# Second softmax pass of an audio tower: bias written into PSUM ahead of the score matmuls, exponential read from PSUM

## The chip, the cores and the metric
One core of one Trainium2 chip runs the whole kernel. The metric is device time in microseconds. Engine names are those of the profile: PE is TensorE's matmul, PEld its weight load, DVE is VectorE, ACT is ScalarE, POOL is GpSimd, SP is the engine that issues most DMAs.

## The reference, cut to what matters
The input x has shape (16, 256, 128): 16 batches. A convolution over 5 time steps gives 252 rows of 256 features per batch; then comes an attention layer with 16 heads of width 16, a learned bias by relative position and a causal mask; then a quantised feed-forward layer. The change touches the attention alone:

```
sim = einsum('bhid,bhjd->bhij', q, k) * scale
sim = sim + bias                  # rel_emb[bucket(j - i)], one 252 x 252 table per head
sim = where(causal_mask, mask_value, sim)
attn = softmax(sim, axis=-1)
out = einsum('bhij,bhjd->bhid', attn, v)
```

The same bias table serves all 16 batches.

## The kernel before
The kernel has three stages in time: a preparation of weights and bias tables (to about 60 us), the convolution and attention of all batches (about 60 to 535 us), and the feed-forward layer (the rest). The first and last are the same in both kernels.

The attention stage is a software pipeline with one **body** per batch, numbered b = -3 to 16. Every engine runs its own list of steps per body, in order: `PE_ORDER` (L439), `DVE_ORDER` (L446), `ACT_ORDER` (L450). A step is a name, an offset and a part; the offset says which batch it works on: `("k", 1, 0)` in body b computes the first half of the k projection of batch b + 1, `("conv", 2, ...)` the convolution of batch b + 2. A step whose batch does not exist is left out, so the bodies at both ends are thinner: body 15 has no P1, q, k, v or conv.

The scores are computed twice. The **first pass** (P1, 12 pieces of 504 columns, for batch b + 1) has queries on partitions. PE puts the bias in with a matmul against an identity and adds q times k (L616, L619), and DVE takes row maxima out of PSUM (`mx`, L758). The maxima are transposed (step mT, L627), negated on ACT (step mneg, L866), and sent by a DMA into row 65 of the stacked q (L961). The **second pass** (P2, 12 pieces, for batch b) has keys on partitions, and that row makes each score come out less its maximum. For each piece PE computes the scores (L637), DVE adds the bias table `biasT` and writes the sum to the SBUF buffer `sbr`, which has four slots (L749), and ACT takes the exponential of `sbr` into `pt` (L834). The step PV (L650, L654) multiplies three pieces of `pt` by v. P2[0] to P2[5] stand at the start of a body, P2[6] to P2[11] at its end.

P1 and P2 pieces share four PSUM banks in turn, in PE's order. Before PE writes a piece, `score_free` (L510) waits until the engine that read the bank four pieces earlier is done: the maximum for a P1 piece, the addition for a P2 piece. Other steps share one more ring of single banks; among them x2T (L690) uses the bank of mT and so waits for mneg.

From the maxima runs this loop round to the next body: P1[11], mT, mneg, DMA, P2[0] on PE, the k projection behind it on PE (L596), its high and low parts kh on ACT (L876) and kl on DVE (L789), three DMAs into the stacked k (L946), and P1[0] of the next batch, which waits for all six DMAs of q and k. On ACT, kh stands behind P2[0], which stands behind everything from the end of the body before: `xh`, `xnh`, `osb`, `xn2`, P2[6], mneg, P2[7], P2[8], `x2`, P2[9], qh, P2[10], `osb`, P2[11].

Step `ax` (L815) takes the largest magnitude of a batch of finished features. In the kernel before no ordinary body has it: one stands behind each of the 12 P2 additions of body 15, and four stand in body 16.

Of the kernel before, what the change touches and what calls it, by code (L numbers as in the profile page):

```python
# [25 lines left out]
ALU = mybir.AluOpType  # L26
# [38 lines left out]
def audio_tower(nc, x, cw, cb, gamma, beta, rmean, rvar, wq, wk, wv, wo, bo, rel, wg, wu, wd, hot, out):  # L65
    with ExitStack() as ctx:
# [3 lines left out]
        def sem(name):  # L70
# [22 lines left out]
            lines_dram bias_in anti_r antib_r flipT_ps flipN_ps biasT_r biasN_r vec_ready cbx_r vec_in ident pool_init dve_init act_init  # L93
            x_in xT_ps xh_r xl_r conv_ps relu_r v1_r h_r hb_r bns_r mv_r ve_r rstd_r nb_r xn_r
            xnT_ps xnh_r xnl_r q_ps k_ps v_ps qh_r ql_r kh_r kl_r va_r stack_in
            p1_ps mx_r mT_ps mneg_r mneg_in p2_ps sb_r exp_r pv_ps osb_r oT_ps rc_r on_r onT_ps onh_r onl_r
            wo_ps h2_r spilled bns2_r mv2_r ve2_r rstd2_r nb2_r nm2_r nm_r xn2_r x2T_ps x2_r ax_r
            xi_r xqh_r xq_r ag_r ared par sc_r ap_r ao_r oq_r oh_r ol_r""".split()
        names += [n + str(i) for n in "g_ps g_r u_ps raw_r raw_out raw_in gq_r sig_r sq_r p_r au_r uq_r g2_r o_r".split()
# [28 lines left out]
        def sba(name, shape, dt=F32):  # L128
            return sb(name, shape, dt, pa)
# [291 lines left out]
        xn, xn2 = sba("xn", [128, 2, C]), sba("xn2", [128, 2, C])  # L421
        xnh, xnl = sba("xnh", [128, KT, N], F16), sba("xnl", [128, KT, N], F16)
        mx = sba("mx", [128, 2, H])
        sbr = sba("sbr", [128, 4, 2 * N])
        pt = sba("pt", [128, 2, 3, 2 * N])
        osb = sba("osb", [128, G, N])
        rc = sba("rc", [128, 2, H])
# [7 lines left out]
        def pieces(kind, off, first, end):  # L435
            return [(kind, off, n) for n in range(first, end)]
# [6 lines left out]
                    ("wo", -1, 1), P1[8], ("v", 1, 1), P1[9], P1[10], ("xT", 3, 0), P1[11], ("PV", 0, 1), ("xnT", 2, 0),  # L443
                    P2[6], P2[7], P2[8], ("mT", 1, 0), ("q", 2, 0), P2[9], ("x2T", -1, 0), P2[10], ("q", 2, 1),
                    P2[11], ("PV", 0, 2)]
        DVE_ORDER = [P2[0], P2[1], ("kl", 1), P2[2], P2[3], P2[4], P2[5], ("on", -1, 0), P1[0], ("on", -1, 1),  # L446
                     P1[1], P1[2], P1[3], P1[4], ("onl", -1), P1[5], P1[6],
                     ("stats", 2), P1[7], ("h2", -1), P1[8], P1[9], ("stats2", -1), P1[10], ("xl", 3), P1[11],
                     ("xnl", 2), P2[6], P2[7], P2[8], P2[9], P2[10], ("ql", 2), P2[11]]
        ACT_ORDER = [P2[0], ("kh", 1), P2[1], ("osb", -1, 3), P2[2], P2[3], P2[4], P2[5], ("osb", 0, 0),  # L450
                     ("relu", 2), ("onh", -1), ("xn", 2), ("va", 1), ("xh", 3), ("xnh", 2), ("osb", 0, 1), ("xn2", -1),
                     P2[6], ("mneg", 1), P2[7], P2[8], ("x2", -1), P2[9], ("qh", 2), P2[10], ("osb", 0, 2), P2[11]]


# [3 lines left out]
        FF_ACT = {(-1, ("relu", 2)): [("ffhi", 0, j) for j in range(6)],  # L458
                  (-1, ("xn", 2)): [("ffhi", 0, j) for j in range(6, FF_BANKS - 1)],
                  (-1, ("va", 1)): [("ffhi", 0, FF_BANKS - 1)]}  # L460
        for c in range(12):
            FF_DVE[B - 1, P2[c]] = [("ax", c - B + 1)]
        for c, at in zip(range(12, B), (("on", -1, 1), ("onl", -1), ("h2", -1), ("stats2", -1))):
            FF_DVE[B, at] = [("ax", c - B)]
        FF_PE = {(-1, P1[2]): [("ffT", 0, 0), ("ffT", 0, 1)]}
        for j in range(FF_BANKS):
            FF_DVE[-1, P1[j + 2]] = [("fflo", 0, j)]
# [42 lines left out]
        def score_free(pe, st, b):  # L510

            i = PIECES.index(st) - 4
            for back in range(5):
                while i >= 0:
                    kind, off, n = PIECES[i]
                    if runs(b - back if isinstance(b, int) else b, off):
                        return wait(pe, "sb_r" if kind == "P2" else "mx_r", 12 * (b - back + off) + n + 1)
                    i -= 4
                i += len(PIECES)

        def piece_heads(n):

# [16 lines left out]
        def pe_step(pe, b, par):  # L539
            odd = 1 - par  # L540
            for st in step_order(PE_ORDER, FF_PE, b):
# [88 lines left out]
                elif name == "P2":  # L630
                    if part == 0:
                        wait(pe, "mneg_in", 16 * (c + 1))
                    score_free(pe, st, b)
                    heads, w = piece_heads(part)
                    kt = slice(TT, N) if w == TT else slice(0, TT)
                    for n, hd in enumerate(heads):
                        last = nc.tensor.matmul(ps[0:TT, score_bank[name, part], n * w:(n + 1) * w],  # L637
                                                kS[par][0:P2_ROWS, hd, kt], qS[par][0:P2_ROWS, hd, N - w:N],
                                                start=True, stop=True)
                    last.then_inc(S["p2_ps"], 1)  # L640
                elif name == "PV":
                    g, vc = part, va[odd if off else par]
                    if isinstance(c, int) and c == 0:
                        wait(pe, "ff_lo", FF_BANKS)
                    wait(pe, "exp_r", 12 * c + 3 * (g + 1))
                    wait(pe, "va_r", c + 1)
                    wait(pe, "osb_r", 4 * c + g - 1)
                    p = pt[0:TT, g % 2]
                    for i in range(4):
                        nc.tensor.matmul(ps[32 * i:32 * i + 32, OB + g % 2, 0:N], vc[0:TT, 0, 4 * g + i, :],  # L650
                                         p[:, i // 2, (i % 2) * N:(i % 2) * N + N], start=True, stop=True,
                                         skip_group_check=True)
                    for i in range(4):
                        last = nc.tensor.matmul(ps[32 * i:32 * i + 32, OB + g % 2, TT:N],  # L654
                                                vc[0:TT, 1, 4 * g + i, :], p[:, 2, i * TT:(i + 1) * TT],
                                                start=False, stop=True, skip_group_check=True)
                    last.then_inc(S["pv_ps"], 1)
                elif name in ("OT0", "OT1"):
                    t = int(name[2])
                    wait(pe, "osb_r", 4 * (c + 1))  # L660
                    misc_free(pe, name, b)
                    for g in range(G):
                        last = nc.tensor.transpose(bank[0:TT, g * 128:(g + 1) * 128],  # L663
                                                   osb[:, g, t * TT:(t + 1) * TT], identf[:])
                    last.then_inc(S["oT_ps"], 1)
                elif name == "onT":
                    wait(pe, "on_r", 2 * (c + 1))
                    misc_free(pe, name, b)
                    for k in range(KT):
                        for t in range(2):  # L670
                            last = nc.tensor.transpose(bank[:, k * N + t * TT:k * N + (t + 1) * TT],
                                                       on[0:TT, t, k * 128:(k + 1) * 128], identf[0:TT, 0:TT])
                    last.then_inc(S["onT_ps"], 1)
                elif name == "wo":
                    if part == 0:
                        wait(pe, "onh_r", c + 1)
                        wait(pe, "onl_r", c + 1)
                        misc_free(pe, name, b)
                    rows = slice(part * TT, (part + 1) * TT)
                    last = three(bank[0:TT, part * C:(part + 1) * C],  # L680
                                 [((onh[:, k, rows], onl[:, k, rows]), (woT[:, 0, k], woT[:, 1, k]))
                                  for k in range(KT)])
                    if part == 1:
                        last.then_inc(S["wo_ps"], 1)
                elif name == "x2T":
                    wait(pe, "xn2_r", 2 * (c + 1))
                    misc_free(pe, name, b)
                    for k in range(KT):
                        for t in range(2):
                            last = nc.tensor.transpose(bank[:, k * N + t * TT:k * N + (t + 1) * TT],  # L690
                                                       xn2[0:TT, t, k * 128:(k + 1) * 128], identf[0:TT, 0:TT])
                    last.then_inc(S["x2T_ps"], 1)
# [15 lines left out]
        def dve_step(dve, b, par):  # L708
            for st in step_order(DVE_ORDER, FF_DVE, b):
# [28 lines left out]
                elif name == "fflo":  # L738
# [2 lines left out]
                    nc.vector.scalar_tensor_tensor(bank_dst(group, 1)[0], ps[:, OB + st[2] % 2, :],  # L741
                                                   winv[:, group[0][4]:group[0][4] + 1], bank_dst(group, 0)[0],
                                                   ALU.mult, ALU.subtract).then_inc(S["ff_lo"], 1)
                elif name == "P2":
                    n = st[2]
                    heads, w = piece_heads(n)
                    wait(dve, "p2_ps", 12 * c + n + 1)
                    wait(dve, "exp_r", 12 * c + n - 3)
                    nc.vector.tensor_tensor(sbr[0:TT, n % 4].rearrange("p (h w) -> p h w", w=w),  # L749
                                            ps[0:TT, score_bank[name, n], 0:2 * N].rearrange("p (h w) -> p h w", w=w),  # L750
                                            biasT[0:TT, heads[0]:heads[-1] + 1, 0:w], ALU.add).then_inc(S["sb_r"], 1)
                elif name == "P1":
                    n = st[2]
                    heads, w = piece_heads(n)
# [64 lines left out]
        def act_step(act, b, par):  # L819
            odd = 1 - par  # L820
            for st in step_order(ACT_ORDER, FF_ACT, b):
# [7 lines left out]
                                         scale=winv[:, group[0][4]:group[0][4] + 1]).then_inc(S["ff_hi"], 1)  # L829
                elif name == "P2":  # L830
                    n = st[2]
                    wait(act, "sb_r", 12 * c + n + 1)
                    wait(act, "pv_ps", 4 * c + n // 3 - 1)
                    nc.scalar.activation(pt[0:TT, n // 3 % 2, n % 3], sbr[0:TT, n % 4], ACT.Exp  # L834
                                         ).then_inc(S["exp_r"], 1)
                elif name == "osb":
                    g = st[2]
                    wait(act, "pv_ps", 4 * c + g + 1)
# [619 lines left out]
```

## Time and profile before

| | us |
|---|---|
| median of 3 runs | 842.63 |
| range of the runs | 839.97 to 850.68 |
| profiled execution | 847.05 |
| its span, first to last instruction | 845.2 |

Over the span PE is busy 73%, DVE 72%, ACT 51%, POOL 22%. These shares are means over stages with different limits: between 100 and 480 us PE is busy 9 tenths or more of nearly every slice, while between 490 and 535 us no engine is.

### The profile page before, as it was taken

What the parts mean: (1) busy time and instruction counts of PE and PEld (TensorE: products, weight loads), DVE (VectorE), ACT (ScalarE), POOL (GpSimd) and SP (SyncE); (2) the same over time, 40 slices, a digit from 0 to 9 for tenths busy, and PEclk for the clock granted to TensorE, in tenths of its full rate; (3) what the DMA queues carried; (4) which work ended last, traced back from release to release, by engine and by line L of the source; (5) the groups of instructions that cost most, each with busy time, mean ns of one, the idle gap of its engine ahead of it and who ended that gap; (6) DMA issues with size and microseconds to landing.
All of it is one profiled execution on the core that took longest, in us unless ns stands there. A gap on an engine that the chain in (4) does not pass through costs nothing. (4 is left out here: it accounts for less than half of the span.)

```text
span 845.2 us, 15311 instructions
## 1 busy us (share of the span) xinstructions
PE 617.8 (73%) x5162; PEld 463.7 (55%) x5162; DVE 610.1 (72%) x949; ACT 432.7 (51%) x622; POOL 187.6 (22%) x239
## 2 busy tenths in 40 slices
PE   2535699899999999999999865399997720002998
PEld 1224577778777777787777643144443300002998
DVE  5736777778887788887788756256679995995442
ACT  0510444666545665545665343144498862444772
POOL 1320222112221122221122000000035552650000
PEclk9976999999999999999999865599999975555999
DMA  6333023232133331233321200000043302661343
GB/s 169 100 124 44 15 32 58 45 58 42 29 56 44 56 56 31 38 56 44 56 48 27 41 1 12 13 0 0 0 170 158 149 37 73 219 220 49 115 131 98
DMA packets 40063, 57.37 MB, mean 68 GB/s; under 512 B 5820, under 2 KB 31868, under 8 KB 40028
## 3 DMA queue, kind: packets, MB, share of 16 engines
q1 hardware_dynamic: 38876, 56.13, 26.7%
q10 hardware_dynamic: 1152, 0.79, 0.5%
q8 instruction: 20, 0.33, 0.2%
q14 instruction: 15, 0.12, 0.1%
HBM read 25.06 MB, written 19.13 MB: 52 GB/s over the span
## 5 line engine op out<-in xcount | busy, mean ns | idle before, releaser
L758 DVE TENSOR_REDUCE mx<-ps 126x2 f32<-126x504 f32 (+1 forms) x192 | 125.1, 675 | 45.0 <-PE ps L619 44.5
L1406 PE MATMUL ps<-wdT,oh 128*126 128x256 f16 x384 | 65.7, 279 | 93.6 <-DVE ol L1366 93.6
L834 ACT ACTIVATE pt<-sbr 126x504 f32<-126x504 f32 x192 | 115.1, 617 | 30.5 <-DVE sbr L749 29.3
L749 DVE TENSOR_TENSOR sbr<-ps,biasT 126x504 f32<-126x504 f32 x192 | 120.6, 674 | 9.9 <-PE ps L637 9.3
L1406 PEld LDWEIGHTS ps<-wdT,oh 128*126 128x126 f16 x384 | 48.6, 140 | 94.5 <-DVE ol L1366 94.5
L616 PE MATMUL ps<-biasN,identb 126*126 126x504 bf16 x192 | 75.2, 392 | 21.1 <-DMA k_st<-kl 21.1
L910 POOL TENSOR_TENSOR h<-h,bc 126x512 f32<-126x512 f32 x16 | 20.3, 1268 | 273.5 <-ACT h L850 273.5
L619 PE MATMUL ps<-k_st,q_st 65*126 65x252 f16 (+1 forms) x512 | 75.3, 249 | 0.0
L1077 PE MATMUL ps<-x2t,wgT 128*128 (+1 forms) x288 | 63.9, 387 | 11.0 <-DVE x2t L1120 11.0
L1077 PE MATMUL ps<-x2t,wuT 128*128 (+1 forms) x288 | 63.4, 376 | 11.2 <-ACT raw L1246 11.1
L637 PE MATMUL ps<-q_st,k_st 66*126 66x252 f16 (+1 forms) x512 | 67.5, 252 | 3.3 <-DMA q_st<-mneg 3.3
L619 PEld LDWEIGHTS ps<-k_st,q_st 65*126 65x126 f16 x512 | 60.9, 140 | 16.0 <-issue 1.5
L573 PE MATMUL ps<-wcT,xh 128*126 128x256 f16 x320 | 62.2, 279 | 0.0
L637 PEld LDWEIGHTS ps<-q_st,k_st 66*126 66x126 f16 x512 | 50.6, 139 | 11.2 <-issue 6.2
L861 ACT ACTIVATE xn<-h,nb,rstd 126x256 f32<-126x256 f32 x32 | 17.5, 593 | 72.7 <-POOL nb L904 72.7
L1077 PEld LDWEIGHTS ps<-x2t,wgT 128*128 128x128 f16 x288 | 28.7, 100 | 46.0 <-DVE x2t L1120 11.4
L1406 PE MATMUL ps<-wdT,ol 128*126 128x256 f16 x192 | 53.5, 279 | 0.0
L1077 PEld LDWEIGHTS ps<-x2t,wuT 128*128 128x128 f16 x288 | 27.6, 98 | 46.8 <-issue 9.0
L1284 POOL TENSOR_SCALAR sq<-sig 128x1512 int32<-128x1512 f32 x16 | 44.1, 2759 | 39.2 <-ACT sig L1255 32.2
L841 ACT ACTIVATE osb<-ps 128x252 f32<-128x252 f32 x64 | 23.7, 370 | 52.7 <-PE ps L663 43.2
L1266 ACT ACTIVATE g<-gat,sc 128x1512 int16 (+1 forms) x16 | 24.8, 1554 | 44.5 <-DVE gat L1183 33.0
L573 PE MATMUL ps<-wcT,xl 128*126 128x256 f16 x160 | 44.9, 281 | 0.0
(181 smaller groups left out, 1430.5 us busy)
## 6 DMA issues: line engine op xcount, KB each, us to landing
up_raw<-raw SPq DMA_DIRECT2D x14, 756.0 KB, 3.2
raw<-up_raw SPq DMA_DIRECT2D x14, 756.0 KB, 4.3
q_st<-qh SPq DMA_DIRECT2D x32, 128.0 KB, 3.9
k_st<-kh SPq DMA_DIRECT2D x32, 128.0 KB, 4.0
res<-hall SPq DMA_DIRECT2D x16, 252.0 KB
hin<-res SPq DMA_DIRECT2D x16, 252.0 KB
out<-y SPq DMA_DIRECT2D x16, 252.0 KB
xin<-in_x SPq DMA_DIRECT2D x16, 128.0 KB, 3.7
```

Of the source, the lines that this page charges most:

```text
L573: last = nc.tensor.matmul(bank[0:TT, t * C:(t + 1) * C], *products[i], start=False, stop=(i == 14))
L616: nc.tensor.matmul(dst, identb[0:TT, 0:TT], biasN[0:TT, heads[0]:heads[-1] + 1, N - w:N], start=True, stop=True)
L619: last = nc.tensor.matmul(dst[:, n * w:(n + 1) * w], qS[odd][0:P1_ROWS, hd, qt], kS[odd][0:P1_ROWS, hd, 0:w], start=False, stop=True, skip ...
L637: last = nc.tensor.matmul(ps[0:TT, score_bank[name, part], n * w:(n + 1) * w], kS[par][0:P2_ROWS, hd, kt], qS[par][0:P2_ROWS, hd, N - w:N] ...
L749: nc.vector.tensor_tensor(sbr[0:TT, n % 4].rearrange("p (h w) -> p h w", w=w), ps[0:TT, score_bank[name, n], 0:2 * N].rearrange("p (h w) - ...
L758: nc.vector.tensor_reduce(mx[0:TT, 0 if w == TT else 1, heads[0]:heads[-1] + 1], ps[0:TT, score_bank[name, n], 0:2 * N].rearrange("p (h w) ...
L834: nc.scalar.activation(pt[0:TT, n // 3 % 2, n % 3], sbr[0:TT, n % 4], ACT.Exp).then_inc(S["exp_r"], 1)
L841: nc.scalar.activation(osb[:, g], ps[:, OB + g % 2, 0:N], ACT.Copy).then_inc(S["osb_r"], 1)
L1077: last = nc.tensor.matmul(ps[:, 3 * hf + j, 0:2 * N], w[:, wp, k, m], rhs, start=(i == 0), stop=(i == 5))
L1266: nc.scalar.activation(g2[hf][:], unit(2 * turn(i) + hf), ACT.Copy, scale=col["inv_p"]).then_inc(S[f"g2_r{hf}"], 1)
L1284: nc.gpsimd.tensor_scalar(sq[hf][:], sig[hf][:], 65536.0, 0.0, ALU.mult, ALU.add).then_inc(S[f"sq_r{hf}"], 1)
L1406: last = nc.tensor.matmul(ps[0:TT, s, t * C:(t + 1) * C], o[par][:, m, rows], wdT[:, w, m], start=(m == 0 and i == 0), stop=(m == MT - 1 a ...
```

## The change
The buffer `sbr` and DVE's addition go. In their place, a step `seed` copies the bias of a P2 piece into the piece's PSUM bank as soon as the bank is free, ahead of the matmul. DVE does pieces 0 to 5, 10 and 11, ACT pieces 6 to 9. PE adds the scores to what stands in the bank (`start=False`), and ACT takes the exponential straight from PSUM. A bank that held a P2 piece is now free when its exponential is done. The seeds of P2[0] to P2[3] are made at the end of the body before. The `ax` steps are spread: one in each body, two bodies late, and the last one in body 16.

```diff
-        sbr = sba("sbr", [128, 4, 2 * N])
...
-        DVE_ORDER = [P2[0], P2[1], ("kl", 1), P2[2], P2[3], P2[4], P2[5], ("on", -1, 0), P1[0], ("on", -1, 1),
+        SEED, SEED_NEXT = pieces("seed", 0, 0, 12), pieces("seed", 1, 0, 4)
+        BY_ACT = range(6, 10)
+        DVE_ORDER = [("kl", 1), SEED[4], SEED[5], ("on", -1, 0), ("ax", -2), P1[0], ("on", -1, 1),
                      P1[1], P1[2], P1[3], P1[4], ("onl", -1), P1[5], P1[6],
                      ("stats", 2), P1[7], ("h2", -1), P1[8], P1[9], ("stats2", -1), P1[10], ("xl", 3), P1[11],
-                     ("xnl", 2), P2[6], P2[7], P2[8], P2[9], P2[10], ("ql", 2), P2[11]]
+                     ("xnl", 2), SEED[10], SEED[11], SEED_NEXT[0], ("ql", 2)] + SEED_NEXT[1:4]
         ACT_ORDER = [P2[0], ("kh", 1), P2[1], ("osb", -1, 3), P2[2], P2[3], P2[4], P2[5], ("osb", 0, 0),
-                     ("relu", 2), ("onh", -1), ("xn", 2), ("va", 1), ("xh", 3), ("xnh", 2), ("osb", 0, 1), ("xn2", -1),
+                     ("relu", 2), ("onh", -1), ("xn", 2), ("va", 1), ("xh", 3), SEED[6], SEED[7], SEED[8], ("xnh", 2),
+                     SEED[9], ("osb", 0, 1), ("xn2", -1),
                      P2[6], ("mneg", 1), P2[7], P2[8], ("x2", -1), P2[9], ("qh", 2), P2[10], ("osb", 0, 2), P2[11]]
...
-        for c in range(12):
-            FF_DVE[B - 1, P2[c]] = [("ax", c - B + 1)]
-        for c, at in zip(range(12, B), (("on", -1, 1), ("onl", -1), ("h2", -1), ("stats2", -1))):
-            FF_DVE[B, at] = [("ax", c - B)]
+        FF_DVE[B, ("stats2", -1)] = [("ax", -1)]
...
-                        return wait(pe, "sb_r" if kind == "P2" else "mx_r", 12 * (b - back + off) + n + 1)
+                        return wait(pe, "exp_r" if kind == "P2" else "mx_r", 12 * (b - back + off) + n + 1)
...
+        def seed(eng, st, b):
+            _, off, n = st
+            score_free(eng, ("P2", 0, n), b + off)
+            heads, w = piece_heads(n)
+            to = ps[0:TT, score_bank["P2", n], 0:2 * N].rearrange("p (h w) -> p h w", w=w)
+            bias = biasT[0:TT, heads[0]:heads[-1] + 1, 0:w]
+            if n in BY_ACT:
+                nc.scalar.activation(to, bias, ACT.Copy).then_inc(S["act_seed"], 1)
+            else:
+                nc.vector.tensor_copy(to, bias).then_inc(S["dve_seed"], 1)
...
-                    score_free(pe, st, b)
+                    seeded(pe, c, part)
...
-                                                start=True, stop=True)
+                                                start=False, stop=True, skip_group_check=True)
...
-                    wait(act, "sb_r", 12 * c + n + 1)
+                    wait(act, "p2_ps", 12 * c + n + 1)
                     wait(act, "pv_ps", 4 * c + n // 3 - 1)
-                    nc.scalar.activation(pt[0:TT, n // 3 % 2, n % 3], sbr[0:TT, n % 4], ACT.Exp
+                    nc.scalar.activation(pt[0:TT, n // 3 % 2, n % 3], ps[0:TT, score_bank["P2", n], 0:2 * N], ACT.Exp
                                          ).then_inc(S["exp_r"], 1)
```

`seeded` waits on `act_seed` or `dve_seed` for the piece's own seed.

## Rows read from the trace of the kernel before

**Rows 1.** Busy time by stretch: PE, PEld, DVE, ACT, POOL, then PEclk, DMA share, GB/s.
```profile
200.00:300.00 100.00, 92.39 (x952) 77.25 (x951) 82.24 (x162) 57.08 (x112) 22.57 (x40) 1.00 0.29 45
```
**Rows 2.** Waits of PE between 200 and 400 us: total us, times, longest.
```profile
PE ps L616 <- DMA k_st<-kl: 7.9, 8, 1.0
PE ps L690 <- ACT mneg L866: 3.8, 8, 0.5
PE ps L627 <- DVE mx L758: 3.0, 8, 0.4
```
**Rows 3.** Groups by line on ACT, 120 to 480 us: busy, mean ns, idle before.
```profile
L834 ACT ACTIVATE pt<-sbr 126x504 f32<-126x504 f32 x168 | 100.7, 617 | 22.9 <-DVE sbr L749 21.8
L871 ACT ACTIVATE xnh<-ps 128x504 f16<-128x504 f32 x14 | 8.3, 590 | 8.9 <-PE ps L582 8.9
```
**Rows 4.** The same view for DVE.
```profile
L749 DVE TENSOR_TENSOR sbr<-ps,biasT 126x504 f32<-126x504 f32 x168 | 105.0, 674 | 4.3 <-PE ps L637 3.9
```
**Rows 5.** Timeline of ACT, 279 to 306 us: start, length (merged if several), instruction, [idle before].
```profile
279.88 0.35 ACT L866 ACTIVATE mneg<-ps 16x252 f16<-16x252 f32 x1
280.14 1.12 ACT L834 ACTIVATE pt<-sbr 126x504 f32<-126x504 f32 x2
281.17 0.56 ACT L890 ACTIVATE x2t<-ps 128x504 f32 x1
281.64 0.61 ACT L834 ACTIVATE pt<-sbr 126x504 f32<-126x504 f32 x1
282.15 0.66 ACT L876 ACTIVATE qh<-ps,qks 128x504 f16<-128x504 f32 x1
...
284.30 1.30 ACT L834 ACTIVATE pt<-sbr 126x504 f32<-126x504 f32 x2 [0.72 <-DVE sbr L749]
285.50 0.66 ACT L876 ACTIVATE kh<-ps,qks 128x504 f16<-128x504 f32 x1
...
301.90 0.36 ACT L845 ACTIVATE xh<-ps 128x256 f16<-128x256 f32 x1
302.92 0.59 ACT L871 ACTIVATE xnh<-ps 128x504 f16<-128x504 f32 x1 [0.66 <-PE ps L582]
...
303.81 1.09 ACT L861 ACTIVATE xn<-hall,nb,rstd 126x256 f32 x2
...
305.60 0.35 ACT L866 ACTIVATE mneg<-ps 16x252 f16<-16x252 f32 x1
```
**Rows 6.** Timeline of PE in the same body.
```profile
280.38 0.62 PE L690 MATMUL ps<-identf,xn 126*128 126x126 f32 x4 [0.47 <-ACT mneg L866]
...
282.81 0.43 PE L637 MATMUL ps<-q_st,k_st 66*126 66x252 f16 x2
...
284.38 0.38 PE L637 MATMUL ps<-q_st,k_st 66*126 66x252 f16 x2
...
290.35 0.40 PE L654 MATMUL ps<-pt,va 126*32 126x126 f32 x8
291.71 0.43 PE L616 MATMUL ps<-biasN,identb 126*126 126x504 bf16 x1 [0.97 <-DMA k_st<-kl]
```
**Rows 7.** DMA issues: count, KB each, median us from issue to landing.
```profile
q_st<-mneg SPq DMA_DIRECT2D x16, 8.0 KB, 1.8
```
**Rows 8.** Timeline of DVE in bodies 15 and 16, 484 to 536 us.
```profile
491.10 0.68 DVE L749 TENSOR_TENSOR sbr<-ps,biasT 126x504 f32<-126x504 f32 x1 [1.08 <-PE ps L637]
491.70 0.67 DVE L815 TENSOR_REDUCE amax_x<-x2t 128x1 f32<-128x504 f32 x1
...
498.15 0.25 DVE L797 RECIPROCAL rc<-ps 126x16 f32<-126x16 f32 x1
...
527.54 0.67 DVE L815 TENSOR_REDUCE amax_x<-x2t 128x1 f32<-128x504 f32 x1
```
**Rows 9.** Timeline of PE in body 15.
```profile
493.94 0.66 PE L663 MATMUL ps<-identf,osb 128*126 128x128 f32 x4 [0.48 <-ACT osb L841]
...
499.01 1.08 PE L663 MATMUL ps<-identf,osb 128*126 128x128 f32 x4 [3.32 <-DVE on L799]
```
**Rows 10.** Timeline of ACT in body 15.
```profile
514.82 0.62 ACT L834 ACTIVATE pt<-sbr 126x504 f32<-126x504 f32 x1 [0.28 <-DVE sbr L749]
```

More of the change, by code:

```diff
@@ L95, in audio_tower @@
             xnT_ps xnh_r xnl_r q_ps k_ps v_ps qh_r ql_r kh_r kl_r va_r stack_in
-            p1_ps mx_r mT_ps mneg_r mneg_in p2_ps sb_r exp_r pv_ps osb_r oT_ps rc_r on_r onT_ps onh_r onl_r
+            p1_ps mx_r mT_ps mneg_r mneg_in p2_ps act_seed dve_seed exp_r pv_ps osb_r oT_ps rc_r on_r onT_ps onh_r onl_r
             wo_ps h2_r spilled bns2_r mv2_r ve2_r rstd2_r nb2_r nm2_r nm_r xn2_r x2T_ps x2_r ax_r
@@ L516, in score_free, with seeded @@
                     if runs(b - back if isinstance(b, int) else b, off):
-                        return wait(pe, "sb_r" if kind == "P2" else "mx_r", 12 * (b - back + off) + n + 1)
+                        return wait(pe, "exp_r" if kind == "P2" else "mx_r", 12 * (b - back + off) + n + 1)
                     i -= 4
                 i += len(PIECES)
+        def seed(eng, st, b):
[8 more added lines that the diff above has]
+                nc.vector.tensor_copy(to, bias).then_inc(S["dve_seed"], 1)
+        def seeded(pe, c, n):
+            if n in BY_ACT:
+                wait(pe, "act_seed", len(BY_ACT) * c + n - BY_ACT[0] + 1)
+            else:
+                wait(pe, "dve_seed", (12 - len(BY_ACT)) * c + n + 1 - (len(BY_ACT) if n > BY_ACT[0] else 0))
         def piece_heads(n):
@@ L743, in dve_step @@
                                                    ALU.mult, ALU.subtract).then_inc(S["ff_lo"], 1)
[L744 to L751, printed above, removed]
+                elif name == "seed":
+                    seed(dve, st, b)
                 elif name == "P1":
@@ L831, in act_step @@
                     n = st[2]
-                    wait(act, "sb_r", 12 * c + n + 1)
+                    wait(act, "p2_ps", 12 * c + n + 1)
                     wait(act, "pv_ps", 4 * c + n // 3 - 1)
-                    nc.scalar.activation(pt[0:TT, n // 3 % 2, n % 3], sbr[0:TT, n % 4], ACT.Exp
+                    nc.scalar.activation(pt[0:TT, n // 3 % 2, n % 3], ps[0:TT, score_bank["P2", n], 0:2 * N], ACT.Exp
                                          ).then_inc(S["exp_r"], 1)
+                elif name == "seed":
+                    seed(act, st, b)
                 elif name == "osb":
```

## The prediction, made before the changed kernel was run
> **What bounds the kernel now.** I read first how busy each engine is by stretch, since the change lives in one stage. Inside the pipeline, 100 us hold 92.39 us of PE work at the full granted clock, against 82.24 on DVE and 57.08 on ACT [rows 1]. So the two engines that the change relieves and loads are not the resource that is full, and what can be won in an ordinary body is PE's waiting. The view of PE's waits names nearly all of it: 14.7 us in the 200 us that hold 8 bodies, over half of it P1[0] waiting for the last DMA of the stacked k, the rest x2T waiting for mneg and mT waiting for the last maximum [rows 2]. One body lasts 25.72 us, from one mneg to the next [rows 5], so 1.84 us of each is such waiting.
>
> The largest wait closes a loop: mneg, DMA, P2[0], k, kh, kl, DMA, P1[0], maxima, mneg. The timeline of ACT shows why P1[0] is late: from xh on, ACT is nearly solid until kh, and kh stands behind exponentials which themselves wait for DVE's additions, 21.8 us over 14 bodies [rows 3], in this body 0.72 us just ahead of P2[11] and P2[0] [rows 5]. So the question is whether kh, and with it P1[0], comes earlier or later in the new order.
>
> **The change, part by part.** I walk one body on ACT from the end of xh to kh. Steps are differences of starts, which are shorter than the durations shown, since instructions overlap. An exponential out of SBUF takes steps of 0.515 us (280.14 to 281.17 is two), a 504-column instruction out of PSUM 0.47 (x2 at 281.17, next at 281.64), mneg 0.26 (279.88 to 280.14) [rows 5].
>
> - The four ACT seeds. No row shows ACT writing PSUM. Lower bound 0.47 each, as x2; upper bound 0.62, the full duration of an exponential [rows 3]. I take 0.51, the step of the ACT instruction that reads SBUF: 2.04 us added.
> - The exponentials read PSUM. I take 0.47; they could stay at 0.515.
> - New walk. ACT is free after xh at 301.90 + 0.27 = 302.17. Then four seeds 2.04, xnh 0.47, two osb 0.26 each as mneg has the same 252 columns, xn2 twice 0.50, seven exponentials (P2[6] to P2[11], P2[0]) 3.29, mneg 0.26, x2 0.47, qh 0.66 less 0.1 overlap: 8.61 us. So ACT could start kh at 310.78. Before, kh starts at 285.50 + 25.72 = 311.22 [rows 5]. The 2.04 us of seeds are paid by waits that go: xnh for its transposes (0.66, in all 14 bodies 8.9 us [rows 3]) and the waits for additions.
> - PE and the mneg DMA move too. mneg now has the seeds ahead of it: 302.17 + 2.04 + 0.47 + 0.26 + 1.00 + 0.47 = 306.41 against 305.60, **0.81 us later**, with x2T, q's second half and P2[11] queued behind it on PE. x2T starts at 280.38 + 25.72 + 0.81 = 306.91; P2[0] follows it by 2.43 us as now [rows 6], at 309.34. The DMA (8 KB, median 1.8 us to landing [rows 7]) leaves at about 306.8 and lands at 308.6, so it is still covered by that work; were it to land 2.6 us after issue or more, P2[0] and the k projection would wait for it. k is done 1.57 us after P2[0] starts [rows 6], 310.9, with a hand-over 311.0. This is later than ACT's 310.78, so PE sets kh: 311.0, **0.2 us earlier** than now.
> - P1[0] then has its k 0.2 us earlier. Its other condition is PE itself: P2[0] to the end of PV is 290.35 + 0.40 - 282.81 = 7.94 us of work [rows 6], 317.28. Now P1[0] starts at 291.71 + 25.72 = 317.43. **Gain 0.15 to 0.2 us a body**; over the 15 steps from body to body 2.6 us. PE's wait at P1[0] does not vanish for nothing: it is spent at x2T instead.
> - DVE. Twelve additions of 0.674 go [rows 4], eight copies come. No row shows a copy from SBUF to PSUM. Bounds: half an addition, 0.34, since it reads one tensor instead of two, and a whole one, 0.67. I take 0.6, the step of the addition, which has the same length. They hide: P2[10] and P2[11] are seeded while ACT runs mneg to x2, SEED_NEXT in the gaps around ql. Two queues count. kl stands behind SEED_NEXT[3], which waits for the exponential P2[11]: that ends near 310.4, the copy near 311.1, kl is wanted at about 311.7: 0.6 us of cover. P2[4] and P2[5] stand behind kl: seeded by 313.6, wanted on PE near 314. One ax a body (0.67 [rows 8]) falls in DVE's idle time ahead of P1[0], free.
> - PE's second pass has the same matmuls; accumulating costs nothing visible, as the first pass does it already.
> - **The end of the stage.** In body 15 nothing else fills the engines. DVE alternates an addition and an ax, 0.6 us each [rows 8], so the on step behind the six pairs starts at 498.15 although its transposes were done at 493.94 + 0.66 = 494.60, and PE stands 3.32 us for it [rows 8, 9]. With neither on DVE, on starts at about 494.7: 3.45 us. The second half of that body loses at least the 0.28 us wait of the last exponential [rows 10], and in body 16 the ax between h2 and the statistics (527.54, 0.6 us of step [rows 8]) goes. Together 4.3 us, with 1 more if all of the second half's waits for additions go.
>
> Sum: 2.6 + 4.3 = 6.9 us, from 847.05 us of the profiled execution to 840.1. That execution lies 4.4 us over the median of the three runs; taken from 842.63 the forecast is **835.7 us**.
>
> **A rule weighed against it.** PE never stands for a P2 bank in the rows of its waits [rows 2], while the change holds every bank longer: from the seed, through the matmul, to the end of the exponential. The Trainium skill, "Perfetto Trace Analysis", section "Optimization Strategy", says that the same gap repeating on the engine that should be saturated can mean that too little PSUM is there for the next tile. By that rule the four banks would show a new repeating gap on PE, and the time would be that of the third rival; nothing in the trace of before can show it.
>
> **The rivals.**
> 1. *Half or all of PE's listed waits go* (15%). For it: DVE has room, and the waits lie at joints that the change touches. All of them would give 15 x 1.84 + 4.3 = 32 us, **811**, half of them 18 us, 824.5. Against: mneg gets later, not earlier, and the largest wait has a DMA in it.
> 2. *Nothing in the bodies, the end alone* (18%). Exponentials no cheaper (7 x 0.045), seeds at 0.62 (4 x 0.11): kh at 311.5, 0.3 us later than now. Between nothing and that, the bodies cost 0 to 4.5 us and the end gives 4.3: **838 to 843**. In this case the change does not speed the second pass, but only clears DVE at the end.
> 3. *The bank ring becomes the limit* (10%), the case on the slower side. Place: P2[6] to P2[9], then P2[10] to P2[1], then P2[2] to P2[5], each round seeded only after the exponentials of the one before. Price of a turn: seed 0.67 [rows 4], matmuls 0.43 [rows 6], three hand-overs of about 0.15 (mneg's end to x2T): 1.55 us, twice a body, 3.1, less the 1.56 us a body that exponentials wait now [rows 3]: 1.5 a body, 23 us, less 4.3: **861**. It decides once ACT has no other work to put between an exponential and the one four pieces on, or a seed stands on DVE behind ql or kl by more than the 0.6 us of cover. Against: between P2[6] and P2[10] ACT has six other instructions.
>
> **The numbers.** Forecast 57%, rivals 15, 18 and 10. The forecast's own range goes down to 832 (seeds at 0.47 bring mneg and all behind it 0.16 us earlier, 2.4 us in 15 bodies, and the end gives 1 more) and up to 838, where rival 2 begins. The range for 8 in 10 takes in both, the near edge of rival 1 and, above, costs in the bodies of up to 0.7 us, more than twice rival 2's: **824 to 849**. Two per cent, about what a measurement of this kernel can tell from no change, is 17 us. Faster than 825.8: rival 1 and 0.02 of the forecast, 0.17. Slower than 859.5: rival 3, 0.10. Within: 0.73.
>
> **What would show it.** Right: the pitch from mneg to mneg 25.3 to 25.7 us; mneg 0.8 us later after xh; x2T waiting 1.2 us or more; P1[0] waiting under 0.9; on in body 15 some 3.5 us earlier after its transposes; the ACT seed near 0.5 us of step. Wrong: a PE wait on a seed in every body (rival 3), P2[0] waiting for the mneg DMA in most bodies, or kl late behind SEED_NEXT[3].

## The result, and the profile after

The changed kernel is slower, by less than one per cent: 853.85 us (median of 4 runs, 851.49 to 856.57) against 845.7 us for the kernel before on the same chip (median of 4), a ratio of 1.0088 with a 95% interval of 1.0055 to 1.0122. The ratios here and below are estimated over the single runs and differ a little from the quotients of the medians. The forecast was 835.7 us. The profiled execution took 856.57 us with a span of 854.6 us, against 847.05 and 845.2: 9.4 us of span to explain.

The first view is the summary of the instruction mneg, which every body has once: count, shortest, median and longest duration in ns, and the first and last start in us. Kernel before, then the changed kernel:

```profile
L866 ACT ACTIVATE mneg<-ps x16: 352/353/369, 100.7 to 486.8; 16x252 f16<-16x252 f32 x16
```
```profile
L880 ACT ACTIVATE mneg<-ps x16: 352/352/369, 100.7 to 498.9; 16x252 f16<-16x252 f32 x16
```

The first mneg falls at the same time in both. The 15 bodies to the last one take 398.2 us in place of 386.1, **26.55 us a body in place of 25.74: 12.1 us lost**. Behind the last mneg the span runs another 355.7 us in place of 358.4: **2.7 us won**. The sum is the 9.4 us.

The mean over the 15 bodies holds for the ordinary body too: the eight in the middle take (419.63 - 207.32) / 8 = 26.54 us in the changed kernel and (408.57 - 202.67) / 8 = 25.74 in the kernel before. At the ends the bodies differ by other amounts. The largest is from the second mneg to the third, 27.7 us against 25.3, at a mean granted clock of PE of 0.95 against 1.00.

The price of the instructions is not the reason. The groups of the changed kernel by line (busy us, mean ns, idle before):

```profile
L846 ACT ACTIVATE pt<-ps 126x504 f32<-126x504 f32 x192 | 105.8, 589 | 4.2 <-PE ps L655 3.9
...
L530 DVE COPY ps<-biasT 126x504 f32<-126x504 f32 x128 | 81.0, 678 | 27.2 <-ACT pt L846 26.7
```

The exponential out of PSUM takes 589 ns (617 out of SBUF [rows 3]) and waits almost nowhere any more: over the run it is idle 4.2 us, where 14 bodies alone had 22.9 [rows 3]. The copy on DVE, 678 ns, costs what the addition did [rows 4].

The timeline of ACT in one body of the changed kernel, to be held against [rows 5]:

```profile
280.91 1.09 ACT L875 ACTIVATE xn<-h,nb,rstd 126x256 f32<-126x256 f32 x2 [4.71 <-POOL nb L918]
...
282.48 0.37 ACT L859 ACTIVATE xh<-ps 128x256 f16<-128x256 f32 x1
282.74 1.61 ACT L528 ACTIVATE ps<-biasT 126x504 f32<-126x504 f32 x3
...
284.75 0.59 ACT L528 ACTIVATE ps<-biasT 126x504 f32<-126x504 f32 x1
...
286.97 0.35 ACT L880 ACTIVATE mneg<-ps 16x252 f16<-16x252 f32 x1
...
289.18 0.68 ACT L890 ACTIVATE qh<-ps,qks 128x504 f16<-128x504 f32 x1
...
291.67 0.68 ACT L890 ACTIVATE kh<-ps,qks 128x504 f16<-128x504 f32 x1
...
307.40 1.09 ACT L875 ACTIVATE xn<-h,nb,rstd 126x256 f32<-126x256 f32 x2 [4.62 <-POOL nb L918]
```

From xh to mneg it takes 4.49 us, before 305.60 - 301.90 = 3.70 [rows 5]: the seeds put mneg 0.79 us later. To hold the rest together I count from the start of xn, the last point ahead of the change's first instruction. That is 280.91 here; in the body of [rows 5] it is 300.33, from this row of the kernel before:

```profile
300.33 1.09 ACT L861 ACTIVATE xn<-h,nb,rstd 126x256 f32<-126x256 f32 x2 [4.62 <-POOL nb L904]
```

kh starts 10.76 us after xn, before 285.50 + 25.72 - 300.33 = 10.89: **not later**. Small differences need care here, since the bodies alternate. In the kernel before, counted from the xn of the body ahead, kh starts 285.50 - 274.70 = 10.80 us behind it:

```profile
274.70 1.09 ACT L861 ACTIVATE xn<-h,nb,rstd 126x256 f32<-126x256 f32 x2 [4.71 <-POOL nb L904]
```

P1[0], the first q move and the last k move, read below from 300.33, come out 0.09 us shorter from this row too: 17.01, 8.13 and 12.72. In the changed kernel kh alternates between 10.76 and 10.85, so like against like it is only 0.04 us earlier. And yet P1[0] is late, as PE's timeline shows:

```profile
287.47 0.62 PE L708 MATMUL ps<-identf,xn 126*128 126x126 f32 x4 [0.72 <-ACT mneg L880]
...
289.90 0.43 PE L655 MATMUL ps<-q_st,k_st 66*126 66x252 f16 x2
...
298.78 0.43 PE L634 MATMUL ps<-biasN,identb 126*126 126x504 bf16 x1 [0.95 <-DMA k_st<-kl]
```

P1[0] starts 17.87 us after xn, before 291.71 + 25.72 - 300.33 = 17.10 [rows 6]: 0.77 us later (0.86 against 17.01), which is the loss of 0.81 us a body. PE still stands 0.95 us for the last k move, though kl was sent no later. What changed is seen in SP's timeline, which shows the issue of each DMA and which the prediction did not use. Kernel before:

```profile
282.83 1.22 SPq L946 DMA_DIRECT2D q_st<-qh  x2
284.11 0.60 SPq L946 DMA_DIRECT2D q_st<-ql  x1
286.19 1.19 SPq L946 DMA_DIRECT2D k_st<-kh  x2
287.42 0.61 SPq L946 DMA_DIRECT2D k_st<-kl  x1
```

The changed kernel:

```profile
289.88 1.22 SPq L960 DMA_DIRECT2D q_st<-qh  x2
291.16 0.60 SPq L960 DMA_DIRECT2D q_st<-ql  x1
292.38 1.19 SPq L960 DMA_DIRECT2D k_st<-kh  x2
293.61 0.61 SPq L960 DMA_DIRECT2D k_st<-kl  x1
```

The last k move leaves 12.70 us after xn, before 12.81; from there to P1[0] it is now 5.17 us, before 4.29. The first **q** move leaves 8.97 us after xn, before 8.22: 0.75 us later (0.84 against 8.13). It leaves when qh is done, and qh starts on ACT 289.18 - 286.97 = 2.21 us behind mneg with no idle time just before it, in [rows 5] 2.27: ACT's own order hands the delay of mneg on to qh. And from the first q move to P1[0] it is 298.78 - 289.88 = **8.90 us**, before 291.71 - 282.83 = **8.88 us**. The six moves of 128 KB run as one stream; what counts is when it begins. The times from issue to landing (all data in place) show it. For the k moves between 280 and 360 us, shortest, median and longest, kernel before, then the changed kernel:

```profile
DMA to landing us min/median/max: 3.5/4.0/4.3
```
```profile
DMA to landing us min/median/max: 4.3/4.9/5.1
```

In the kernel before the k moves are issued 3.36 to 4.59 us behind the first q move, in the changed kernel 2.50 to 3.73 us. In both they land 6.8, 8.0 and 8.9 us behind it, about one microsecond after each other: issued sooner behind q, they land no sooner. The view by stretch shows that in the changed kernel the stream fills the DMA engines (the last three numbers of a row are PE's clock, the DMA share and GB/s):

```profile
291.00:293.00 2.00, 2.00 (x27) 1.60 (x28) 2.00 (x4) 1.74 (x4) 0.00 (x0) 1.00 0.87 160
293.00:295.00 2.00, 2.00 (x30) 1.80 (x22) 1.31 (x3) 1.65 (x4) 0.00 (x0) 1.00 1.16 117
295.00:297.00 2.00, 2.00 (x23) 1.83 (x21) 1.07 (x3) 0.85 (x2) 0.00 (x0) 1.00 1.16 113
```

From 291 to 297 us the share is 0.87 to 1.16 without a break. So the k moves, sent while the q moves are still under way, wait their turn, and a later q moves the end of k. In the kernel before there is room left in the middle of the stream; this stretch lies as far behind its first q move as 293 to 295 us does above:

```profile
286.00:288.00 2.00, 2.00 (x28) 1.88 (x21) 1.80 (x3) 1.38 (x4) 0.00 (x0) 1.00 0.62 96
```

There the k moves hardly waited for q; experiment e2 measures how little.

### The profile page after: what moved, and what is told of

The parts are those of the page before. It is cut to its first block and busy times, and to the rows that moved or that the text cites. A ratio compares the mean times of both kernels' runs of the same rounds, so it can differ in the third digit from the quotient of the medians.

```text
span 854.6 us, 15158 instructions
## 1 busy us (share of the span) xinstructions
PE 628.3 (74%) x5162; PEld 464.6 (54%) x5162; DVE 574.9 (67%) x885; ACT 452.2 (53%) x686; POOL 184.2 (22%) x239
## 3 DMA queue, kind: packets, MB, share of 16 engines
q1 hardware_dynamic: 38876, 56.13, 28.2%
## 5 line engine op out<-in xcount | busy, mean ns | idle before, releaser
L846 ACT ACTIVATE pt<-ps 126x504 f32<-126x504 f32 x192 | 105.8, 589 | 4.2 <-PE ps L655 3.9
L530 DVE COPY ps<-biasT 126x504 f32<-126x504 f32 x128 | 81.0, 678 | 27.2 <-ACT pt L846 26.7
L655 PE MATMUL ps<-q_st,k_st 66*126 66x252 f16 (+1 forms) x512 | 76.3, 260 | 5.6 <-DVE ps L530 1.8
L1091 PEld LDWEIGHTS ps<-x2t,wuT 128*128 128x128 f16 x288 | 27.6, 98 | 46.7 <-issue 9.7
```

Source lines behind the costliest of these rows:

```text
L530: nc.vector.tensor_copy(to, bias).then_inc(S["dve_seed"], 1)
L846: nc.scalar.activation(pt[0:TT, n // 3 % 2, n % 3], ps[0:TT, score_bank["P2", n], 0:2 * N], ACT.Exp).then_inc(S["exp_r"], 1)
L1091: last = nc.tensor.matmul(ps[:, 3 * hf + j, 0:2 * N], w[:, wp, k, m], rhs, start=(i == 0), stop=(i == 5))
```

## The experiments

**Theory A:** P1[0] comes 8.9 us after the first q move is issued, unless kl or PE is later still. The seeds delay mneg on ACT and qh behind it; mneg also delays x2T, and behind x2T stand q's second half and P2[11] on PE; the first q move follows. **Theory B:** the seeds make the moves themselves slow, since copies by DVE and ACT get in the DMA's way, and q's time does not matter. The kernel before was run again beside each experiment, with 848.5 us beside e1 to e4 and 846.93 us beside e5 to e9, and every ratio is to it; the changed kernel was not run beside them.

**e1: q early in the new kernel.**
```diff
-  ("mT", 1, 0), ("q", 2, 0), P2[9], ("x2T", -1, 0), P2[10], ("q", 2, 1), P2[11], ("PV", 0, 2)]          # PE
+  ("mT", 1, 0), ("q", 2, 0), ("q", 2, 1), P2[9], ("x2T", -1, 0), P2[10], P2[11], ("PV", 0, 2)]
-  ("xnl", 2), SEED[10], SEED[11], SEED_NEXT[0], ("ql", 2)] + SEED_NEXT[1:4]                             # DVE
+  ("xnl", 2), SEED[10], SEED[11], ("ql", 2)] + SEED_NEXT[0:4]
-  P2[6], ("mneg", 1), P2[7], P2[8], ("x2", -1), P2[9], ("qh", 2), P2[10], ("osb", 0, 2), P2[11]]        # ACT
+  P2[6], ("mneg", 1), P2[7], ("qh", 2), P2[8], ("x2", -1), P2[9], P2[10], ("osb", 0, 2), P2[11]]
```
Expected: 

> The new kernel with the second half of the q projection moved on PE from behind P2[10] to right behind the first half, qh on ACT from behind P2[9] to behind P2[7], ql on DVE ahead of SEED_NEXT[0]. Theory A (the six 128 KB moves of q and k are one stream: the last lands 8.9 us after the first q move is issued, whenever k's are issued, and P1[0] waits for it): the first q move leaves about 0.8 us earlier, bounded by P2[11] on PE, whose buffer it overwrites; P1[0] comes 0.8 us earlier, the body lasts 25.7 to 25.8 us in place of 26.55, 15 bodies give 11 to 12 us: 842 us, ratio to the kernel before about 0.995. Theory B (the seeds make the moves themselves slow: copies by DVE and ACT get in the way of the DMA, so the last k move lands 4.9 us after its issue in place of 4.0, and q's time does not matter): kh and kl come when they came, nothing changes, 853 us, ratio 1.008.


Measured: 847.34 us, ratio to the kernel before 0.9975 (0.9943 to 1.0006). All of the slowdown is gone; the eight bodies in the middle take 25.73 us each, before 25.74. The issues on SP and the row of P1[0]:
```profile
283.81 1.22 SPq L960 DMA_DIRECT2D q_st<-qh  x2
...
288.30 0.60 SPq L960 DMA_DIRECT2D k_st<-kl  x1
...
292.69 0.43 PE L634 MATMUL ps<-biasN,identb 126*126 126x504 bf16 x1 [0.16 <-DMA k_st<-kl]
```
Here xn starts at 275.62: the first q move leaves after 8.19 us, 0.78 earlier, and P1[0] starts 8.88 us behind it. kl leaves after 12.68 us, when it left before, and now its 4.39 us suffice. B expected nothing to change.

**e2: the same in the kernel before** (ql on DVE to behind P2[8]).
```diff
-  ("xnl", 2), P2[6], P2[7], P2[8], P2[9], P2[10], ("ql", 2), P2[11]]
+  ("xnl", 2), P2[6], P2[7], P2[8], ("ql", 2), P2[9], P2[10], P2[11]]
```
Expected: 

> The kernel before with the same move of q's second half, qh and ql to an earlier place. Theory A: the first q move leaves up to 1 us earlier; the gain per body is what PE's wait at P1[0] leaves, 0.6 to 0.95 us, unless kl becomes the bound (issue 12.81 us after xn plus at least 3.3 us of landing, against 17.10 now): 15 bodies give 9 to 14 us, ratio 0.983 to 0.990. Theory B: kl is issued when it was, nothing changes, ratio 1.00.


Measured: 841.72 us, ratio 0.9927 (0.9901 to 0.9953), a smaller gain than A's smallest, 0.990. The reason is A's own exception, k's chain:
```profile
280.48 1.22 SPq L946 DMA_DIRECT2D q_st<-qh  x2
...
286.10 0.60 SPq L946 DMA_DIRECT2D k_st<-kl  x1
...
290.22 0.43 PE L616 MATMUL ps<-biasN,identb 126*126 126x504 bf16 x1 [0.60 <-DMA k_st<-kl]
```
The q moves now leave 5.62 us ahead of kl, and P1[0] comes 9.74 us after the first of them but 4.12 us after kl: with the stream begun early enough, kl alone decides. The body lasts 25.4 us. This also shows how close the two limits lie in the kernel before: kl needs 4.12 us to P1[0] when q is out of its way, and has 4.29 there, so q held P1[0] back by only 0.17 us a body. The larger part of e2's gain is that kl itself leaves sooner, 286.10 - 273.66 = 12.44 us after xn, where the like body of the kernel before has 12.72.

**e3: q late in the kernel before.** No seed is in this kernel.
```diff
-  P2[9], ("qh", 2), P2[10], ("osb", 0, 2), P2[11]]        # ACT
+  P2[9], P2[10], ("qh", 2), ("osb", 0, 2), P2[11]]
-  P2[10], ("ql", 2), P2[11]]                              # DVE
+  P2[10], P2[11], ("ql", 2)]
```
Expected: 

> The kernel before with qh on ACT one exponential later (behind P2[10]) and ql on DVE behind P2[11]'s addition, so that k's chain is not held up by it. No seed is in this kernel. Theory A: the first q move leaves 0.5 us later, the body grows by 0.5 us to 26.2, 15 bodies cost 7.5 us, ratio 1.009, and the last k move lands later after its issue than the 4.0 us of the kernel before. Theory B: kl is issued no later (P2[11]'s addition no longer stands behind ql, so kh can be up to 0.7 us earlier) and lands after 4.0 us as before: no change or up to 0.7 us a body faster, ratio 0.988 to 1.00.


Measured: 859.61 us, ratio 1.0139 (1.0095 to 1.0183). This rebuilds the slowdown without the change. The summaries of mneg and of the k moves:
```profile
L866 ACT ACTIVATE mneg<-ps x16: 353/353/370, 101.7 to 497.7; 16x252 f16<-16x252 f32 x16
...
DMA to landing us min/median/max: 3.6/4.6/5.6
```
The issues on SP and the row of P1[0]:
```profile
291.75 1.22 SPq L946 DMA_DIRECT2D q_st<-qh  x2
...
295.76 0.61 SPq L946 DMA_DIRECT2D k_st<-kl  x1
...
300.66 0.43 PE L616 MATMUL ps<-biasN,identb 126*126 126x504 bf16 x1 [1.50 <-DMA k_st<-kl]
```
The body grows to 396.0 / 15 = 26.40 us. xn starts at 283.11 here, so kl leaves after 12.65 us, no later than in the kernel before (12.72 in the like body), but its landing is later: 4.90 us to P1[0], and 8.91 us from the first q move. The second row above is the landing time of the k moves, 4.6 us at the median; it is 4.0 in the kernel before and 4.9 in the changed one. A landing that slow without any seed is what B excludes. The ratio is over A's 1.009. The eight bodies in the middle take 26.24 us, 0.5 more than before, as A had it; the mean of 26.40 comes from two bodies between 127 and 183 us that take 27.6 and 28.2 us, at a mean granted clock of 0.94, where the kernel before has 1.00. Why the clock is lower there was not tried.

**e4: the ax steps alone**, in the kernel before.
```diff
-  P2[5], ("on", -1, 0), P1[0], ("on", -1, 1),
+  P2[5], ("on", -1, 0), ("ax", -2), P1[0], ("on", -1, 1),
-        for c in range(12):
-            FF_DVE[B - 1, P2[c]] = [("ax", c - B + 1)]
-        for c, at in zip(range(12, B), (("on", -1, 1), ("onl", -1), ("h2", -1), ("stats2", -1))):
-            FF_DVE[B, at] = [("ax", c - B)]
+        FF_DVE[B, ("stats2", -1)] = [("ax", -1)]
```
Expected: 

> The kernel before with one part of the change alone: the ax steps spread over the bodies, as in the new kernel. Both theories: nothing in the ordinary bodies (ax falls in DVE's idle time ahead of P1[0]); at the end DVE's six pairs of addition and ax in body 15 become six additions, on comes 3 us earlier, and the ax between h2 and the statistics in body 16 goes: 2.7 to 4.3 us faster, ratio 0.995 to 0.997.


Measured: 844.24 us, ratio 0.9946 (0.9916 to 0.9976): 4.6 us of 848.5, at the upper end of what was expected. In the profile the body lasts 25.76 us, as before, and 3.9 us are won behind the last mneg (354.5 us to the end, before 358.4). The spread ax is a gain by itself. Whether it is larger alone than in the whole change is not shown: from the last mneg to the feed-forward's first matmul, single profiles give 543.44 - 489.97 = 53.5 us here, 552.82 - 498.87 = 54.0 in the changed kernel and 543.70 - 486.80 = 56.9 before.

**e5: one move fewer** in the new kernel; qh goes into the stacked q once, and the product of q's high and k's low part is left out.
```diff
-  (("q", qS[odd], ((qh, (0, 2)), (ql, (1,)))),
+  (("q", qS[odd], ((qh, (0,)), (ql, (1,)))),
```
Expected: 

> The new kernel with five moves a body in place of six: qh is moved into the stacked q once, not twice, so the product of q's high part and k's low part is left out. Theory A (one stream of moves sets P1[0]): the stream gets shorter by one move, about 1.2 us of the 8.9; P1[0] then comes as early as PE is ready, 0.95 us earlier, the body lasts 25.6 us, 14 us less, 840 us, ratio about 0.991; the last k move lands 4.0 us or less after its issue. Theory B (seeds slow the moves): each move is as slow as before, the last k move lands 4.9 us after its issue, 853 us, ratio 1.008.


Measured: 836.72 us, ratio 0.9887 (0.9853 to 0.9922), and the k moves land after 3.8 us at the median. P1[0] at 290.54 follows the first q move (282.67) by 7.87 us, and PE no longer stands for it in most bodies. The body lasts (485.9 - 98.9) / 15 = 25.80 us. All seeds are still there.

**e7: no seeds on ACT**; P2[6] to P2[9] wait for their banks on PE and go without their bias.
```diff
-  ("xh", 3), SEED[6], SEED[7], SEED[8], ("xnh", 2), SEED[9], ("osb", 0, 1), ("xn2", -1),
+  ("xh", 3), ("xnh", 2), ("osb", 0, 1), ("xn2", -1),
-                wait(pe, "act_seed", len(BY_ACT) * c + n - BY_ACT[0] + 1)
+                score_free(pe, ("P2", 0, n), c)
```
Expected: 

> The new kernel without the four seeds on ACT: P2[6] to P2[9] wait for their banks on PE and add to what stands there, so their bias is left out. Theory A: mneg, x2T, P2[11] and qh lose the 0.8 us that the seeds put ahead of them; the first q move leaves 0.7 us or more earlier after xn, the body falls from 26.55 to 25.5 to 25.9 us, 10 to 15 us less: 839 to 844 us, ratio 0.990 to 0.997. Theory B: 8 of 12 copies remain, so the moves stay slow (4.6 us or more to landing), at most 5 us less: 848 us or more, ratio above 1.002.


Measured: 835.9 us, ratio 0.9899 (0.9847 to 0.9951); the body lasts (480.5 - 101.1) / 15 = 25.29 us. With xn at 271.50:
```profile
276.44 0.35 ACT L880 ACTIVATE mneg<-ps 16x252 f16<-16x252 f32 x1
...
278.65 0.68 ACT L890 ACTIVATE qh<-ps,qks 128x504 f16<-128x504 f32 x1
...
279.36 1.22 SPq L960 DMA_DIRECT2D q_st<-qh  x2
...
288.27 0.43 PE L634 MATMUL ps<-biasN,identb 126*126 126x504 bf16 x1 [0.96 <-DMA k_st<-kl]
```
mneg comes 4.94 us after xn in place of 6.06, the first q move after 7.86 in place of 8.97, and P1[0] 8.91 us behind it. So the four seeds on ACT are what made q late. The landing of k stays at 4.9 us, since q and k moved together. B's ratio above 1.002 lies outside the interval.

**e8: the kernel before with q early, k early and ax spread.** e1's PE and ACT edits, e2's, e4's, and:
```diff
-  PE_ORDER = [P2[0], ("k", 1, 0), ("k", 1, 1), P2[1],
+  PE_ORDER = [("k", 1, 0), ("k", 1, 1), P2[0], P2[1],
-  ACT_ORDER = [P2[0], ("kh", 1), P2[1],
+  ACT_ORDER = [("kh", 1), P2[0], P2[1],
```
Expected: 

> The kernel before with q's second half, qh and ql early, with the k projection ahead of P2[0] on PE and kh ahead of P2[0] on ACT, and with ax spread. Theory A: with q early the bound is k's own chain (kl issued 12.4 us after xn, P1[0] 4.1 us behind it); k ahead of P2[0] brings kh 0.5 us earlier and P1[0] with it, as PE's wait of 0.6 us there allows. Body 25.0 us in place of 25.7, 11 us, and 4.5 for ax: ratio 0.978 to 0.985. Theory B: k earlier alone gives the 0.5 us a body, 7.5 us, and ax 4.5: ratio 0.986.


Measured: 828.14 us, ratio **0.978** (0.9746 to 0.9813): faster than the kernel before, and by its ratio than the changed one. B's 0.986 lies outside the interval. The body lasts 24.85 us.

**e9: the new kernel with q and k early.** The PE and ACT edits of e8's fence, and:
```diff
+  ("mT", 1, 0), ("q", 2, 0), ("q", 2, 1), ("x2T", -1, 0), P2[9], P2[10], P2[11], ("PV", 0, 2)]                        # PE
+  SEED[6], SEED[7], SEED[8], ("xnh", 2), ("xn2", -1), P2[6], ("mneg", 1), P2[7], SEED[9], P2[8],                      # ACT
+  ("qh", 2), ("x2", -1), ("osb", 0, 1), P2[9], P2[10], ("osb", 0, 2), P2[11]]
+  DVE_ORDER = [("kl", 1), SEED[3], SEED[4], SEED[5], ... ("xnl", 2), SEED[10], SEED[11], ("ql", 2)] + SEED_NEXT[0:3]  # DVE
```
Expected: 

> The new kernel with the same two moves, and ACT's order ahead of q changed: xn2, P2[6], mneg directly behind xnh, SEED[9] behind P2[7], osb behind x2; kl on DVE ahead of SEED[3]. Theory A: the first q move leaves 7.6 us after xn in place of 8.97, P1[0] can come at 16.5 us in place of 17.9, the body lasts 25.1 to 25.4 us, 17 us less than the new kernel: 834 to 838 us, ratio 0.985 to 0.991. Theory B: only k's 0.5 us or less, 846 us, ratio 0.999.


Measured: 837.49 us, ratio 0.9908 (0.9875 to 0.9941). The body lasts 25.14 us, so with q and k early the changed second pass runs below the 25.74 of the kernel before. It stays behind e8, whose interval lies wholly below. One place is seen, in the view of waits of the weight loads between 150 and 450 us (total us, times, longest):
```profile
PEld ps L655 <- ACT ps L528: 10.6, 40, 0.3
```
Weight loads of P2 stand 10.6 us for ACT's seeds, just under 0.9 us in each of the 12 bodies; e8 has no such wait on ACT. How much of the 0.29 us a body this makes was not separated.

## Why the prediction was wrong, point by point

**The step that failed** is the one on P1[0]: "P1[0] then has its k 0.2 us earlier." It took the time from kl's issue to its landing as fixed and let kh decide. From kl's issue to P1[0] it took 5.17 us in place of 4.29. The runs show that the first q move decides: 8.88 us in the kernel before, where kl's own limit is only 0.17 us short of it (e2), 8.90 in the changed kernel, 8.88 in e1, 8.91 in e3 and e7. The first q move left 0.75 to 0.84 us later against xn, and the body grew by 0.81. The prediction had the delay in hand: it put mneg 0.81 us later "with x2T, q's second half and P2[11] queued behind it on PE", and qh stands behind mneg in its own walk on ACT, but it followed these queues to P2[0] and k, and not to qh, the three q moves and the stream that they begin.

**The sum.** -2.6 us were forecast for the bodies and +12.1 came; -4.3 for the end and -2.7 came; together -6.9 against +9.4 in the profiled executions. Seeds and exponentials were priced well: the step of a seed is 0.51 us (three in 1.61, the last of them 0.59 long) as taken, that of an exponential out of PSUM 0.47 (286.50 to 286.97) as taken, the copy on DVE like the addition as taken (0.678 against 0.674 long).

**mneg, x2T, P2[0].** mneg 0.79 us later (0.81 forecast); P2[0] on PE 8.99 us after xn, before 282.81 + 25.72 - 300.33 = 8.20 [rows 6], so 0.79 later; the mneg DMA lands after 1.8 us and is covered. PE was ready for P1[0] at 298.78 - 0.95 = 297.83, 16.92 us after xn, where the 317.28 of the prediction puts it at 16.95: this condition was right. x2T stands 0.72 us for mneg, where over 1.2 was expected: PE is late already, since q's first half waits for xnl, which waits for xnh behind the seeds.

**kh and kl.** kh 0.04 us earlier, like body against like (0.2 forecast). kl was not held behind SEED_NEXT[3]: it starts on DVE at 292.40, when kh ends, but with no idle time behind the seeds, so of the 0.6 us of cover nothing was left. Its direction was right and did not matter: with q out of the way, in e2 and e8, kl sets P1[0], and moving k there brought the body from 25.4 to 24.85 us (e8, which also spreads ax). No run moves k alone.

**P1[0] waiting under 0.9 us** was named as a sign that the prediction is right. It is 0.95, as before, and this was the sign to read: kl was sent no later and the wait did not shrink.

**The end of the stage.** on in body 15 comes 507.26 - 498.87 = 8.39 us after mneg, before 498.15 - 486.80 = 11.35: 2.96 us of the 3.45 forecast. The second half of that body gives some back, as PE waits there for a seed that itself waits for an exponential:
```profile
521.45 1.27 PE L655 MATMUL ps<-q_st,k_st 66*126 66x252 f16 x6 [0.55 <-DVE ps L530]
```
That is the turn of rival 3, in a stretch where ACT has little other work to put between. By the Trainium skill's rule on repeating gaps ("Perfetto Trace Analysis", section "Optimization Strategy"), too little PSUM for the next tile can show as the same gap over and over on the engine that should be saturated. In the ordinary bodies of this trace the P2 matmuls have no such wait; only their weight loads wait for ACT's seeds, 9.2 us in 31 times between 150 and 450 us, 0.3 us at the most. And e1 wins back the whole loss with the same banks and as many seeds, although its P2 matmuls do wait for DVE's seeds, 3.4 us in that stretch. So lack of PSUM is not what made the kernel slower.

**The rivals.** Rival 1 did not happen. Rival 2 put exponentials and seeds dearer than they came, and had the bodies lose through kh, which was not late. Rival 3 had the right sign, by another mechanism. That PE's largest wait has a DMA in it was written down as an argument against rival 1; it should have been followed to the DMA's queue.

## What to carry to other kernels

The time from a DMA's issue to its landing is not a property of that DMA alone: here six large moves left close together and the last landed a fixed time after the first was issued, until the first left so early (e2, e8) that the last one's own issue decided. So look at which producer starts the stream and not only at the one that is waited for. When instructions are put in front of a step on an in-order engine, follow every queue behind that step to its DMAs, those of another operand included. And measure each candidate chain from the same anchor in kernels whose orders differ: the one whose distance to the waiting instruction stays is the one that decides. Bodies of one kernel cannot tell this, since between 230 and 390 us of the kernel before both distances to P1[0] stay, 8.88 to 8.93 us from the first q move and 4.28 to 4.34 from kl. From the kernel before to the changed one the first stays, 8.88 and 8.90, and the second goes from 4.29 to 5.17.

## What the runs showed of the hardware

- Six moves of 128 KB from SP's queue, the last issued 3.7 to 4.6 us behind the first, end 8.9 us after the first issue: P1[0] follows it by 8.88, 8.90, 8.88, 8.91 and 8.91 us in five kernels (in some bodies before 230 us and in the last ones by up to 9.4 us). With five moves it is 7.87 us (e5). One such move lands after 3.0 us at the least (e5); sent 5.6 us behind the first, kl lands within 4.1 us (e2). Which property of the moves sets the rate, 113 to 160 GB/s in the rows of the changed kernel, was not tried.
- An ACT copy of 504 columns from SBUF to PSUM takes 0.59 us with a step of 0.51; the exponential reading PSUM takes 0.59 with a step of 0.47, reading SBUF 0.617 and 0.515 [rows 3, 5]. A DVE copy of the same size into PSUM takes 0.678 us, no less than the addition of two tensors.
